# Two of VectorE's elementwise products given to GpSimd in the similarity stage of a four-layer image kernel

## The reference

```python
patches = _unfold3x3_reflect(x).reshape(B, C, K2, P)      # the 9 neighbours of every pixel
cn = xc / jnp.maximum(jnp.linalg.norm(xc, axis=1, keepdims=True), EPS_NORM)
pn = patches / jnp.maximum(jnp.linalg.norm(patches, axis=1, keepdims=True), EPS_NORM)
sim = jnp.einsum('bcp,bckp->bkp', cn, pn)                 # cosine to each neighbour
order = jnp.argsort(-sim, axis=1)
wts = jnp.exp(top_sim) * (jnp.arange(K2)[None, :, None] < kvals)
wts = wts / jnp.sum(wts, axis=1, keepdims=True)
out = jnp.einsum('bckp,bkp->bcp', pat_sorted, wts)        # weighted sum over neighbours
enhanced = out + _group_norm(x, gn_weight, gn_bias)       # then a two-layer network and a residual
```

## Time and profile before

| | |
|---|---|
| time, median of 3 runs | 1011.0 us (1010.9 to 1011.95) |
| profiled execution | 1014.24 us, span 1012.0 us |
| VectorE busy | 837.1 us (83%) |
| TensorE busy | 782.5 us (77%), mean granted clock 0.832 |
| GpSimd busy | 580.1 us (57%), none of it between 2.54 and 162 us |
| ScalarE busy | 387.0 us (38%) |

### The profile page before, as it was taken

The page is one execution under the profiler, slowest core; times in us unless marked ns, Lnnn a source line. Parts: engine busy times, 40 slices in busy tenths (PEclk is TensorE's granted clock), DMA queues, the critical chain, the costliest instruction groups (busy, mean ns, idle before and its releaser), DMA issues.

```text
span 1012.0 us, 8286 instructions
## 1 busy us (share of the span) xinstructions
PE 782.5 (77%) x2365; PEld 377.3 (37%) x2365; DVE 837.1 (83%) x1161; ACT 387.0 (38%) x544; POOL 580.1 (57%) x528
## 2 busy tenths in 40 slices
PE   2345875677787688676788787869379999999997
PEld 1132322222222124534454444423264444444443
DVE  3889842789999858879998899985989998979884
ACT  1120046854454136311212121101049586776650
POOL 0000000076765037877777777777777777777774
PEclk9666987979999889567777677776559999999998
DMA  5000017000000361111111111128353745444422
GB/s 122 0 0 1 0 31 155 17 0 1 1 1 0 64 133 49 37 52 53 51 50 52 52 49 53 51 64 195 110 139 90 195 136 143 122 123 130 120 65 53
DMA packets 32339, 69.82 MB, mean 69 GB/s; under 512 B 12368, under 2 KB 12624, under 8 KB 31184
## 3 DMA queue, kind: packets, MB, share of 16 engines
q1 hardware_dynamic: 16080, 35.27, 13.2%
q0 software_dynamic: 15360, 31.49, 12.1%
q10 hardware_dynamic: 864, 2.64, 1.2%
HBM read 54.94 MB, written 5.77 MB: 60 GB/s over the span
## 4 chain that ended last, share of the span: by engine, by line
PE 42%; DVE 26%; POOL 7%; issue 6%; ACT 2%; DMA 1%; DVEq 0%; ACTq 0%; POOLq 0%
PE PS L1481 19%; POOL got L780 7%; DVE scratch L1174 6%; PE PS L815 5%; DVE scratch L1100 4%; DVE scratch L1181 3%; PE PS L1057 2%; PE PS L1042 2%; PE PS L1498 2%; DVE prodg L791 2%; PE PS L855 2%; DVE PS L1097 2%; PE PS L1274 2%; DVE prodg L795 1%; PE PS L914 1%
## 5 line engine op out<-in xcount | busy, mean ns | idle before, releaser
L780 POOL DMA_INDIRECT got<-corner_table,idx_slot x405 | 402.8, 995 | 123.4 <-issue 123.4
L1042 PE MATMUL PS<-parts,selb 96*128 96x512 bf16 (+1 forms) x256 | 88.4, 446 | 85.0 <-DVE scratch L1100 45.3
L1057 PE MATMUL PS<-scratch,wt 128*128 128x512 f32 x256 | 146.1, 701 | 0.5 <-DVE scratch L1181 0.5
L1481 PE MATMUL PS<-scratch,UZ 128*128 128x512 f32 (+1 forms) x288 | 133.6, 613 | 2.9 <-DVE scratch L1466 2.9
L780 POOL DMA_INDIRECT got<-corner_table,idx_all x75 | 84.9, 1132 | 60.6 <-DVE prime L1348 38.0
L821 ACT ACTIVATE G<-PS 128x32 f32 (+1 forms) x32 | 6.3, 197 | 250.7 <-PE PS L815 250.6
L815 PE MATMUL PS<-ln_g,w 128*128 128x32 f32 x576 | 101.9, 344 | 0.0
L815 PEld LDWEIGHTS PS<-ln_g,w 128*128 128x128 f32 x576 | 99.3, 268 | 0.0
L1564 POOL MEMSET w<- 128x1152 f32 x1 | 1.1, 1058 | 159.7 <-POOLq L599 159.7
L1042 PEld LDWEIGHTS PS<-parts,selb 96*128 96x128 bf16 x256 | 22.9, 116 | 158.2 <-DVE scratch L1100 59.1
L1458 ACT ACTIVATE scratch<-UZ,knot 128x512 f32<-128x512 f32 (+1 forms) x128 | 81.6, 708 | 0.4
(11 more groups left out here) (350 smaller groups left out, 1354.8 us busy)
## 6 DMA issues: line engine op xcount, KB each, us to landing
UZ<-dense_rows SPq DMA_DIRECT2D x24, 512.0 KB, 4.1
got<-corner_table,idx_slot POOLq DMA_INDIRECT x405, 2.5
UZ<-dense_rows SPq DMA_DIRECT2D x96, 64.0 KB, 2.2
XN<-ln_g SPq DMA_DIRECT2D x6, 256.0 KB, 5.8
got<-corner_table,idx_all POOLq DMA_INDIRECT x75, 2.5
corner_table<-scratch SPq DMA_DIRECT2D x1, 1056.0 KB, 10.4
corner_table<-XN SPq DMA_DIRECT2D x1, 1056.0 KB, 10.4
X<-in_x SPq DMA_DIRECT2D x4, 256.0 KB
```

Of the source, the lines that this page charges most:

```text
L780: pool.indirect_dma_start(got[:, slot, tap, :, :].rearrange("p k c -> p (k c)"), None, tables[b], bass.IndirectOffsetOnAxis(ap=index[:, ta ...
L1042: last = nc.tensor.matmul(PS[:, first + n, :], selb[:, which, j, :], parts[:, bass.ds(i * CHUNK + n * BANK, BANK)], start=True, stop=True)
L1057: last = nc.tensor.matmul(PS[:, 4 + n, :], wt[:, W_SUM:W_SUM + P], dBC[:, j % 2, n * BANK:(n + 1) * BANK], start=False, stop=(j == PAIRS - 1))
L1481: last = nc.tensor.matmul(PS[:, n % 4, :], steps[rows, j, :, :].rearrange("p b c -> p (b c)"), ramps[k][rows, j, :], start=(j == 0), stop= ...
```

## The change

GpSimd gets a list in this Block: the product with the right neighbour, as soon as `gr_ready` is raised, and the product with the row below of j = 2, as soon as `gd_ready` is raised. VectorE's L350 goes and its loop makes j = 1 and 0 only. The two reduces that use GpSimd's products wait for the new semaphore `pool_prods`, at 1 and at 2, the other two for `prods`, at 1 and 2. The tiles stay where they were.

```diff
             with nc.Block() as block:
+                @block.gpsimd
+                def _(pool):
+                    pool.wait_ge(S["gr_ready"], 1)
+                    nc.gpsimd.tensor_tensor(prod[:, 3, 0:W + 1, :], GR[:, 0:W + 1, :], GR[:, 1:W + 2, :], ALU.mult).then_inc(S["pool_prods"], 1)
+                    pool.wait_ge(S["gd_ready"], 1)
+                    below_product(nc.gpsimd, 2).then_inc(S["pool_prods"], 1)
+
...
-                    nc.vector.tensor_tensor(prod[:, 3, 0:W + 1, :], GR[:, 0:W + 1, :], GR[:, 1:W + 2, :], ALU.mult).then_inc(S["prods"], 1)
                     vchain(v, nc.vector.memset(avg[:, :], 0.0))
...
-                    v.wait_ge(S["prods"], 1)
+                    v.wait_ge(S["pool_prods"], 1)
                     vchain(v, nc.vector.tensor_reduce(ER[:, 0:W + 1], prod[:, 3, 0:W + 1, :], AX.X, ALU.add))
...
                     v.wait_ge(S["gd_ready"], 1)
-                    for j in (1, 0, 2):
+                    for j in (1, 0):
                         below_product(nc.vector, j).then_inc(S["prods"], 1)
                     for n, j in enumerate((1, 0, 2)):
                         lo, hi, dx = BELOW[j]
-                        v.wait_ge(S["prods"], n + 2)
+                        if j == 2:
+                            v.wait_ge(S["pool_prods"], 2)
+                        else:
+                            v.wait_ge(S["prods"], n + 1)
                         tell(v, nc.vector.tensor_reduce(VD[:, j, lo:hi], prod[:, j, lo:hi, :], AX.X, ALU.add), S["vd_ready"], n + 1)
```

More of the change, by code:

```diff
@@ L296, in build @@
                      "sim_ready", "exp_done", "rank_done", "signs_ready", "others_ready", "w_ready", "prod_ready", "prod_free", "agg_done", "enh_ready", "h_psum",
-                     "h_ready", "f_psum", "prods", "squared", "cmp_ready", "affine_ready", "affine_done")
+                     "h_ready", "f_psum", "prods", "pool_prods", "squared", "cmp_ready", "affine_ready", "affine_done")
             S = {n: sem("s1_" + n) for n in names}
```

## The result

The changed kernel takes 1017.6 us (median of 7 runs, 1014.9 to 1020.18); the kernel before, in the same session, 1011.95 us (7 runs). The ratio is 1.0054, 95% interval 1.0036 to 1.0073: slower, by half a percent. The forecast was slower by 4.4 us, 1015.4 us, with a range up to 1017.0; the way and the mechanism came as forecast, the median lies 0.6 us above the range. In the experiments one run of e2 (1122.14 us) and one of the kernel before (3117.11 us) are far slower than all others; they count in the medians given, but not in the ratios.

The account below looks back on a forecast made before the run. VectorE's queue was taken to bound the stage, ending at 71.21 us. With 4.57 us of products removed and waits at both GpSimd products, it ends 4.4 us later: 1011.0 + 4.4 = 1015.4 us; range 1013.8 to 1017, for 8 in 10 1009.5 to 1017.

Parts of the forecast that it names:

- The hold: VectorE instructions reading SBUF stand until GpSimd's product ends, at both products; chance 0.66, likeliest 1015.4 us.
- upper bound: Price of VectorE's SBUF instructions beside GpSimd: the whole rest of its product, 4.65 us, each time; the lower bound was nothing.
- both places: VectorE's small 128x1 products beside GpSimd's right-neighbour product, and VectorE's instructions from L360 beside GpSimd's row-below product.
- +4.4 and +3.3: Stage end later by 4.4 us if L360 is held at the second GpSimd product, by 3.3 if only products are.
- the forecast's sum: Stage end with both waits: 63.13 us, plus 1.02, 4.40 and 7.02 us, gives 75.57 us instead of 71.21.
- the first place: Beside GpSimd's right-neighbour product: VectorE stands 4.4 us, saves L350's 2.29, so everything to GD is about 2.2 us later.
- the rounding up: The delay up to GD was rounded up a little, to about 2.2 us, for the chance that L153 already stands.
- Rival A: No wait beside GpSimd at all, or tenths: both VectorE products simply go, -4.6 us, 1006.4 us; chance 0.17.
- B: Only large VectorE instructions wait, small ones slip through: -1.1 or -0.1 us, 1010 to 1011 us; chance 0.12.
- C: GpSimd's first product starts late, after about 6 us by the skill: +1.7 us, in all 1009 to 1013 us; chance 0.05.
- a difference in the span carries to the median unchanged: Last step, from stage to time: the 4.4 us are added whole to the median of 1011.0, giving 1015.4 us.
- may add a microsecond: Allowance for later stages with TensorE at a changing clock, used for the range's high end, 1017 us.

Follow-up runs that it names:

- e2: Kernel before, GpSimd idle, VectorE repeating the channel-mean reduce on 64 and 48 pixels as plain delay: 1017.54 us, ratio 1.0042.
- e4: Kernel before plus 16 trials of GpSimd products beside single VectorE instructions of different operand kinds: one run, 1107.6 us, some 94 us longer by the trials.
- e1: The changed kernel once more, no edit: 1018.18 us (10 runs), ratio 1.0051.
- e3: Changed kernel with both GpSimd products started later, beside VectorE reduces, and the scaling of avg moved behind the reduce to ER: 1009.06 us, ratio 0.9963.

## Why the prediction was right and wrong

**The terms of the stage.** The hold, which had no row in the trace of before, was taken at its upper bound by judgement, and that was right at both places: the held instructions last 4.44 and 4.42 us, 4.28 and 4.22 us longer than before (waits of 4.4 and 4.44 us forecast). The product on GpSimd is 4.56 and 4.58 us (4.65 forecast). That VectorE's L360 (L366 now), one input and 0.20 us, is held too was left open between +4.4 and +3.3; it is held. That L153, and not L154, is the first: GpSimd starts 0.09 us after its release, not 0.24. The third reduce ends 30.43 us after the border copy, 30.76 by the forecast's sum (75.57 - 44.81): +4.03 against +4.36. Of the 0.33 us, 0.16 are the first place (GD comes 2.04 us later, 2.2 forecast: a shorter product, and the rounding up), 0.07 the second product, and 0.15 L366's own 0.20 us, which the sum counts once more behind the hold though it runs out inside it; the two products of VectorE take 4.45 us, 0.05 more than forecast. Rival A (no wait) is ruled out by the durations, B (only large instructions) by L153 and by e4's one-column product, C (late first start) by the 0.09 us. Rival C's 6 us, from the Trainium skill, GPSIMD Engine Reference, 2.1 Instruction dispatch, did not show as a delay; but the ISA instruction (MODIFY_POOL_CONFIG in the trace) stands at 35.2 us, 9.2 us ahead of the first product, so a load of that length could be hidden there, and no run here separates the two.

**The step that failed** is the last, from the stage to the time: "a difference in the span carries to the median unchanged: 1011.0 + 4.4 = 1015.4 us", with "may add a microsecond" for the later stages as the range's upper end. The measured median is 6.6 us above the 1011.0 that the forecast stood on, where 4.4 were forecast. First, that base was the median of 3 runs; with 7 runs in the same session as the changed kernel's it is 1011.95, with 23 and 29 in the later ones 1013.49 and 1013.07. So 0.95 of the 6.6 us is no effect of the change, and 5.65 are left. These 5.65 us would have stayed inside the range's +6; it is the base that puts the median outside, and the range held nothing for it. Second, of the 5.65 us 4.03 lie in the stage, by the profiles, and 1.62 behind it. Together 0.95 + 1.62, less the 0.37 by which the stage came out shorter than 4.4, are the 2.2 us of the miss.

The 1.62 us, medians less profiles, can be placed in part. From the border copy of GR to VectorE's first copy in the third layer (L652 before, L661 after) it is 138.88 - 44.81 = 94.07 us before and 98.95 and 98.97 us in the two profiles of the changed kernel: +4.9 at the end of the layer, not +4.0, of which 0.4 is the longer gap shown with e2 (e2 itself has +4.3 there). The other 0.8 us lies well inside the intervals of the times. e1 shows that the changed kernel alone goes from 1014.68 to 1023.15 us with a stage that repeats to 0.01 us, and e2 that a plain delay of 4.1 us ends at a ratio of 1.0042. With the interval of the first measurement, 3.6 to 7.4 us, and of e1, 3.5 to 6.8, the forecast of 4.4 us for the change alone is not contradicted. The later stages' spread (up to 5.4 us between two profiles of one program) was put at one. What makes those stages longer or shorter from run to run is only narrowed down: the two profiles part between 649 and 708 us and part further in the fourth layer.

Nor does the span carry to the time unchanged. The time outside the span is 2.22 to 2.35 us in the runs on record of the kernel before and of e2, and 1.77 to 1.95 us in those of the kernels with a list for GpSimd in this Block. So 0.4 us of what the change adds to the span does not appear in the time; why is not shown.

## What to carry to other kernels

Work for GpSimd is chosen by what VectorE does at that moment, not by how idle GpSimd is: in these runs it is free beside reduces, instructions with a PSUM operand and reciprocals; beside a product of two SBUF tensors, or a copy of two columns or a tensor_scalar of 64 between SBUF tensors, it stops VectorE for up to its own length, however small VectorE's instruction. In a profile such a hold is looked for in durations, an instruction of 0.16 us that takes 4.4, and not in the waits. When a difference of some microseconds is forecast for a kernel of a millisecond, the base needs more than three runs, and the range has to hold the spread of the part that is not changed; and where the removed work has neighbours that can be reordered, as in e3, the same edit wins 0.37%.

## What the runs showed that was not expected

A copy of 2 columns is held (3.55 us) and one of 1 column is not (0.14 us); a product is held even with one column (3.64 us). VectorE holds GpSimd in the same way: 6.47 us for a product of 4.50. So the two engines do not meet only at semaphores, as the description of the chip at the start has it: no semaphore stands between L153 and GpSimd's product, and it waits 4.3 us. And the busy time of VectorE rose by 3.8 us although 4.6 us of work had been taken from it.
